# Graph attention: the target term of the scores is written by TensorE, and no longer added to the mask by VectorE

## What is computed

```python
def _L2_gnn_ref(node_features, edge_index, W, a):
    src, tgt = (edge_index[0], edge_index[1])
    h = node_features @ W
    s_src = h @ a[:d_out]
    s_tgt = h @ a[d_out:]
    e = jax.nn.leaky_relu(s_src[src] + s_tgt[tgt], negative_slope=0.2)
    m = jax.ops.segment_max(e, tgt, num_segments=N)
    e_exp = jnp.exp(e - m[tgt])
    denom = jax.ops.segment_sum(e_exp, tgt, num_segments=N)
    attention = e_exp / denom[tgt]
    h_prime = jax.ops.segment_sum(h[src] * attention[:, None], tgt, num_segments=N)
    return jax.nn.elu(h_prime)
...
x = _layernorm(x + _L2_gnn_ref(x, edge_index, L2_gnn_W, L2_gnn_a), axis=-1)
```

## Time and profile before

| | us |
|---|---|
| median of 3 runs (lowest, highest) | 15079.31 (15066.46, 15080.45) |
| the profiled execution, whole | 14940.95 |
| its span in the trace | 14939.1 |
| granted TensorE clock, mean of the span | 0.644 |

### The profile page before, as it was taken

The page is one execution under the profiler, slowest core; times in us unless marked ns, Lnnn a source line. Parts: engine busy times, 40 slices in busy tenths (PEclk is TensorE's granted clock), DMA queues, the critical chain, the costliest instruction groups (busy, mean ns, idle before and its releaser), DMA issues.

```text
span 14939.1 us, 182194 instructions
## 1 busy us (share of the span) xinstructions
PE 8307.1 (56%) x46670; PEld 7582.8 (51%) x46671; DVE 6695.0 (45%) x13205; ACT 2723.1 (18%) x6542; POOL 8996.6 (60%) x8046
## 2 busy tenths in 40 slices
PE   5777787765555555578845555563333334333334
PEld 5777777754445444477745554463333333333333
DVE  6444444434444444489945565564222223222223
ACT  0111111101111111266623333340000000000000
POOL 3888888873556655500037777754666664666664
PEclk7666666666666667799967677775555555555555
DMA  4333333332333333332212222221111111111111
GB/s 91 18 18 18 18 18 18 18 51 68 97 96 98 98 99 96 99 100 98 94 47 66 66 68 67 67 65 27 23 23 23 23 23 26 23 23 23 23 23 23
DMA packets 851085, 769.36 MB, mean 51 GB/s; under 512 B 652784, under 2 KB 660804, under 8 KB 848965
## 3 DMA queue, kind: packets, MB, share of 16 engines
q0 software_dynamic: 446272, 333.87, 16.1%
q1 hardware_dynamic: 249485, 294.83, 5.9%
q10 hardware_dynamic: 155282, 140.11, 3.1%
HBM read 569.49 MB, written 197.82 MB: 51 GB/s over the span
## 4 chain that ended last, share of the span: by engine, by line
issue 23%; another core or an unknown queue 19%; PE 18%; POOL 15%; DVE 10%; DMA 8%; DVEq 5%; ACT 1%; ACTq 0%; POOLq 0%; SPq 0%
POOL lane_tab L679 9%; DMA lane_tab<-rows,idx 7%; POOL tab L703 6%; PE ps L1127 3%; PE ps L1153 3%; PE ps L1128 3%; DVEq L469 2%; DVE acc_w L1797 2%; DVEq L458 1%; DVE buf_d L469 1%; PE ps L1192 1%; PE ps L1178 1%; PE ps L1168 1%; PE ps L1113 1%
## 5 line engine op out<-in xcount | busy, mean ns | idle before, releaser
L703 POOL DMA_INDIRECT tab<-gcn_tab,idx x3136 | 2983.1, 951 | 1807.3 <-issue 1232.9
L679 POOL DMA_INDIRECT lane_tab<-rows,idx x1664 | 2598.3, 1561 | 616.8 <-issue 616.8
L703 POOL DMA_INDIRECT tab<-att_tab,idx x1568 | 1739.2, 1109 | 1923.1 <-DVEq L1684 1311.1
L1168 PE MATMUL ps<-tab,buf_d 128*128 x3328 | 795.2, 387 | 2162.6 <-issue 2121.8
L1168 PEld LDWEIGHTS ps<-tab,buf_d 128*128 128x128 f32 x3328 | 781.0, 320 | 2249.3 <-issue 2249.3
L1797 DVE TENSOR_TENSOR acc_w<-acc_w,ps 128x512 f32 x416 | 286.1, 688 | 3395.9 <-remote 3108.7
L693 POOL DMA_INDIRECT buf_b<-src_tab,idx x832 | 825.6, 992 | 749.4 <-ACT idx L813 296.4
L693 POOL DMA_INDIRECT acc_w<-src_tab,idx x832 | 838.0, 1007 | 598.0 <-ACT idx L813 335.1
L1065 PE MATMUL ps<-ident,srcg 128*128 128x128 f32 x3328 | 721.9, 405 | 659.6 <-DVE srcg L1430 655.1
L1168 PE MATMUL ps<-tab,buf_a 128*128 x3328 | 762.8, 424 | 531.7 <-issue 403.3
L1168 PEld LDWEIGHTS ps<-tab,buf_a 128*128 128x128 f32 x3328 | 725.9, 330 | 650.5 <-issue 650.1
(11 more groups left out here) (283 smaller groups left out, 16942.2 us busy)
## 6 DMA issues: line engine op xcount, KB each, us to landing
y_stash<-buf_c SPq DMA_DIRECT2D x208, 512.0 KB
tab<-y_stash SPq DMA_DIRECT2D x208, 512.0 KB, 3.3
aux<-dst_rows ACTq DMA_DIRECT2D x104, 512.0 KB
buf_b<-dst_rows ACTq DMA_DIRECT2D x104, 512.0 KB
tab<-gcn_tab,idx POOLq DMA_INDIRECT x3136
aux<-in_edge_attr_dram ACTq DMA_DIRECT2D x848, 32.0 KB
aux<-in_edge_attr_dram SPq DMA_DIRECT2D x848, 32.0 KB
lane_tab<-rows,idx POOLq DMA_INDIRECT x1664
```

The lines of the kernel that those rows point to most:

```text
L679: pool.indirect_dma_start(lane_tab[k][:, :], bass.IndirectOffsetOnAxis(ap=idx[:, b, u:u + 1], axis=0), rows[:, b, u, 0:D1], None, compute_ ...
L703: pool.indirect_dma_start(to[k][:, u, :], None, table[:, :], bass.IndirectOffsetOnAxis(ap=idx[:, k % RING, u:u + 1], axis=0)).then_inc(row ...
L1168: last = pe.matmul(ps_flat[:, bass.ds(rel[u] + q * 512, D)], g_hot[q][:, u, :], g_ring[:, bass.ds(at[u], D)], start=False, stop=True, skip ...
```

## The change

VectorE's second pass over the mask (L1696) goes. In its place TensorE writes `t_step` into the two score banks before the scores: two products per group of the identity with the group's `t_step` columns, each column repeated 128 times, 512 columns per product and bank. The 8 products of s_src then add to what is there (`start=False`) in place of overwriting it. The wait for the banks (`l2_masked`) stands ahead of the new products, and the wait for the s_src columns (`l2_columns`) behind them. The mask counts one semaphore step per group where it counted two.

```diff
@@ -1231,10 +1231,15 @@
             last.then_inc(s.l2_targets, 1)
 
             def l2_scores(g, q):
+                pe.wait_ge(s.l2_masked, g + 1)
+                pe.sem_inc(s.passed, 1)
+                for c in range(2):
+                    pe.matmul(ps[:, c, :].rearrange("p (k f) -> p k f", f=P), ident[:, :],
+                              bc(t_step[:, bass.ds(g * G + c * (G // 2), G // 2)].unsqueeze(2), [P, G // 2, P]),
+                              start=True, stop=False, skip_group_check=True)
                 pe.wait_ge(s.l2_columns, g + 1)
-                pe.wait_ge(s.l2_masked, g + 1)
                 for u in range(G):
-                    last = pe.matmul(region(u, P), bc(s_cols[:, q % 2, u:u + 1], [P, P]), ident[:, :], start=True, stop=True)
+                    last = pe.matmul(region(u, P), bc(s_cols[:, q % 2, u:u + 1], [P, P]), ident[:, :], start=False, stop=True, skip_group_check=True)
                 last.then_inc(s.l2_scored, 1)
 
             def l2_turns(g, q):
@@ -1692,8 +1697,6 @@
                 mask = l2_dst[q]
                 dve.wait_ge(dst_in[q], turn * 16 + 16)
                 dve.tensor_scalar(mask, mask, ids[:, 0:1], -MASK, ALU.not_equal, ALU.mult).then_inc(s.l2_edges_masked, 1)
-                dve.wait_ge(s.l2_edges_masked, g * 2 + 1)
-                dve.tensor_tensor(mask, mask, bc(step_slice(t_step, g).unsqueeze(2), [P, G, P]), ALU.add).then_inc(s.l2_edges_masked, 1)
 
             def l2_maxima(i, q):
                 g = i * RING + q
@@ -1707,7 +1710,7 @@
                     ins.then_inc(s.l2_chain, 1)
                     dve.wait_ge(s.l2_chain, i * (RING * KL2) + (q * KL2 + k))
 
-                dve.wait_ge(s.l2_edges_masked, g * 2 + 2)
+                dve.wait_ge(s.l2_edges_masked, g + 1)
                 dve.wait_ge(s.l2_scored, g + 3)
                 dve.wait_ge(s.l2_exps, g + 1)
                 dve.tensor_tensor(score, l2_dst[q], regions(0, P), ALU.add).then_inc(s.l2_masked, 1)
```

## The result

| | before, us | changed, us | changed / before [95% interval] |
|---|---|---|---|
| median (lowest, highest) | 15078.41 (15066.46, 15083.62) | 15120.12 (15112.0, 15167.44) | 1.0055 [1.0037, 1.0074] |
| the profiled execution | 14940.95 | 15120.06 | |
| granted TensorE clock, mean of the span | 0.644 | 0.659 | |

The change made the kernel 0.55% slower, where the prediction had 0.9% faster as the likeliest. 15120 lies inside the range given (14800 to 15230), but on the other side of the time before.

What follows compares the result with a forecast made beforehand. The prediction took attention to be bound by GpSimd's gather time plus a tail of compute. 14940.95 - 142 + 13 = 14812 us, scaled by 1.00926 to 14950 us (forecast 14880 to 15040); the range given was 14800 to 15230.

Steps and rivals of the forecast that it cites:

- The held gathers (-142 us): Attention loop: gathers starting during L1696 take 1.76 us instead of 0.95; removing it takes 142 us off GpSimd's time.
- Compute hides behind GpSimd: Attention's smooth stretches: gathers allow a step-group every 10.2 us, TensorE needs 8.6, so its extra work shows only in the tail.
- The first rival: Attention: without L1696's holds compute starves and GpSimd waits for its ring; +187 us, 15270 us scaled; chance 0.27.
- TensorE's group (8.6 us, bounds 7.5 and 9.2): Attention step-group on TensorE with the wide products: 8.6 us, midway between fully hidden and fully added; 0.9 above 7.74.
- the sequencer goes on while the long products run: TensorE's group: reading the places overlaps the wide products, which fill 2.57 us of idle time and cost nothing; 7.5 us.
- The tail (+13 us): Fifteen step-groups after the attention's last gather, each 0.9 us longer on TensorE: 13 us more.
- VectorE (7.74 to 6.5 us if TensorE could follow): Attention step-group: VectorE saves 1.23 us, 255 us in all, taking the smooth pace to 6.5 us if TensorE followed.
- The moved wait and the register instructions: Attention loop: `l2_masked` releases as before; semaphore increments and two register instructions cost below 0.2 us per group, inside 8.6.
- That more than the sum comes back (14833): Attention: compute seldom catches up, so GpSimd's ring waits shrink 60 us and the tail 55; 14833 us scaled; chance 0.14.
- That waits eat what the holds free, at no change (15093): Attention: GpSimd's freed time goes into waits, or L1696 caused no holds; only the tail's 13 us remain; chance 0.12.
- TensorE at the low clock throughout: Attention: TensorE's groups take 13.4 us at the low clock, +346 us, 15430 us scaled; chance 0.05.
- Scaling by the median: Whole kernel: the profiled-execution forecast of 14812 us times 1.00926, median over profiled time, gives 14950 us.

Runs made afterwards that it cites:

- the addition of zeros: The changed kernel with an addition of zeros to the mask, two SBUF operands, where L1696 stood: 15114.54 us, 1.0053 of the kernel before.
- narrow products: The kernel before, VectorE's addition kept, with the two new TensorE products added at 8 columns each and overwritten by the scores: 13346.27 us, ratio 1.001.

## Why the prediction was wrong

**The held gathers (-142 us): right in mechanism and size, wrong in what it was worth.** In the first profile of before I sorted all 1568 gathers by the VectorE instruction that ran when they started. The 186 that started in L1696 took 1734 ns in the mean, the 185 in L1715 1491 ns, the others 953 ns; in L1713, which reads one operand from PSUM, they took 946. So L1696 held up the gathers by 186 x 0.79 = 147 us. In the changed kernel none is left of the first kind. The busy time fell by 189 us, more than 142, since the gathers that start in L1715 (now L1718) also took less, 1242 ns in the mean; on the chip without starvation the gathers take 139 us less from first to last. So the inference of the Trainium skill ("SBUF — State Buffer", section "Who interferes with whom"), that such a pass doesn't hold up the making of descriptors, does not hold here: 1734 against 946 ns.

**"Compute hides behind GpSimd": the step that failed.** The prediction counted some 830 us of starved or waited time and let it follow the gathers: shorter gathers, shorter starvation. Its ground was that "most are ended only by a full ring, which says that their length follows GpSimd and not the other way". The same fact says the opposite. Compute doesn't come back before GpSimd stands still, so making GpSimd quicker only brings the full ring earlier, and the time that compute needs without disturbance has to be found in GpSimd's waits: 128 to 142 us were enough in the two profiles of the kernel before because the holds gave it the rest; without them 371 to 463 us were needed. The first rival said just this, with a threshold (279 us of starved time, where 830 stood in the trace), a sign to watch (waits over 260 us; they were 431) and a chance of 0.27. Its other sign did not come: TensorE's idle time "until issue" between the first and the last gather fell from 874 to 579 us (on the chips of one kind, 796 to 580), and it was VectorE's that rose, from 145 to 233 us. Nor did its time: it had +187 us, and +42 and +138 were measured. By its own numbers it was past its threshold threefold, and the argument that set this aside was the one above. It should have had the greater chance.

**TensorE's group (8.6 us, bounds 7.5 and 9.2): mis-sized, 9.92 us in the tail.** Timeline of TensorE in the changed kernel behind the last gather, three groups in a row:

```profile
10170.11 0.39 PE L1256 MATMUL ps<-ident_b,zero_b 128*128 128x260 bf16 x2
10172.99 3.24 PE L1261 MATMUL ps<-tab,buf_d 128*128 x16 [2.49 <-issue]
10176.03 1.91 PE L1249 MATMUL ps<-ident,buf_a 128*128 128x128 f32 x8
10177.74 3.17 PE L1237 MATMUL ps<-valid_s,ident 128*128 x4
10180.74 1.95 PE L1242 MATMUL ps<-ident,tmp_c 128*128 128x128 f32 x16
10182.52 0.39 PE L1256 MATMUL ps<-ident_b,zero_b 128*128 128x260 bf16 x2
10182.75 1.97 PE L1261 MATMUL ps<-tab,buf_d 128*128 x16
10184.56 1.05 PE L1249 MATMUL ps<-ident,buf_a 128*128 128x128 f32 x8
10185.44 1.89 PE L1237 MATMUL ps<-valid_s,ident 128*128 x4
10187.17 1.95 PE L1242 MATMUL ps<-ident,tmp_c 128*128 128x128 f32 x16
10188.95 0.39 PE L1256 MATMUL ps<-ident_b,zero_b 128*128 128x260 bf16 x2
...
10199.72 0.39 PE L1256 MATMUL ps<-ident_b,zero_b 128*128 128x260 bf16 x2
```

From clearing to clearing (L1256, two products) it is 12.41, 6.43 and 10.77 us. The middle one has no idle time before the sums, and it is one in four: the next such sums start at 10221.44 and 10261.64 us, and the loop is unrolled by four. In the kernel before it was one in four too (9017.33, 9048.10 and 9079.06 us, 31 us apart, four groups). So the piece that I read as "the sequencer goes on while the long products run" had nothing to do with their length: at 10177.74 the wide products take 3.17 us and no idle time follows, at 10195.06 they take 3.04 and 2.48 us follow. And the wide products themselves cost 1.89 us at the high level, 1.73 from start to start, as worked out (1.7), but the group with them also holds pieces at the low level behind its idle time:

```profile
10162.00:10164.00 2.00, 1.75 (x13) 1.75 (x13) 1.68 (x4) 0.00 (x0) 0.00 (x0) 0.81 0.00 0
10164.80:10166.60 1.80, 1.80 (x11) 1.80 (x11) 1.39 (x3) 0.00 (x0) 0.00 (x0) 0.50 0.00 0
...
10168.40:10170.20 1.80, 1.80 (x18) 1.79 (x17) 0.00 (x0) 1.80 (x7) 0.00 (x0) 1.00 0.80 257
```

(busy table of short stretches, changed kernel, columns as in rows 1.) The engine idles 2.48 us, then starts the sums, is granted 0.81 over them and 0.50 over the transposes, and is back at 1.00 for the scores. A group with idle time and all its work at the high level is 9.2 us by the prediction's upper bound (7.47 and 1.7), and one in the kernel with the addition of zeros took 9.10 (10139.68 to 10148.78 us); with such a piece it takes 10.6 to 12.4, without idle time 6.43. The prediction gave at the high level to every group and so had no bound above 9.2, although the same rows show the other level.

**The tail (+13 us): 31 to 34 measured**, fifteen times 2.2 us; with 0.9 for each group it was 13. Sixteen step-groups stood behind the last gather before the change too, not fifteen: the earlier trace rows end at 10110 us, the sixteenth stands at 10115.5. On the chip without starvation there is no tail of this kind, three step-groups behind the last gather.

**VectorE (7.74 to 6.5 us if TensorE could follow): right in that it couldn't.** Without the wide products and without the addition the period is 7.6 us, by 0.15 us shorter than before, so TensorE's 7.5 was the next bound directly below VectorE's 7.7.

**The moved wait and the register instructions: no cost seen.** TensorE's idle time for the columns (L887) before L1242 is 9.7 us in the whole stage; it was 24.0. The kernel with narrow products has both, and its ratio is 1.001 [0.9991, 1.0029] on its chip.

**The other rivals.** That more than the sum comes back (14833) did not happen on chips with starvation, where waits and tail grew. That waits eat what the holds free, at no change (15093), was near in time and right as far as it went. TensorE at the low clock throughout didn't come: its granted clock over the span rose from 0.644 to 0.659.

**Scaling by the median.** Attention took 131 us more in the profile, the median of that chip rose by 42 us, on another chip by 138. The factor 1.00926 was no property of the kernel: as the convolutions' time says, the profile and the median of the kernel before came from executions that are not alike.

**Left open.** What starves the engines while gathers go out undisturbed, and why on some chips only, no run here shows; nor what makes the counts of `l2_sums` late. Why the addition of zeros brings nothing is argued only. And on a chip without starvation the whole change was run, but neither of its parts alone.

**Which kernel to take.** On chips with starvation the kernel before; on those without the changed one, by 1.2%. None of the kernels tried beats both everywhere.

## What to carry to other kernels

Before an edit frees an engine that issues gathers, look whether the others do their work while it issues or while it stands; where they work only in its pauses and stalls, those are supply, and freeing it moves its time into waits. If stretches end only with a full ring, ask whether the producer is the bound at all, however busy it is. Price an engine's group over as many groups as the loop is unrolled, at both clock levels that its rows show, and compare a small gain on more than one chip. Before two profiles are compared, compare a stage in them that the change leaves alone.

## What the runs showed of the hardware

- **The kernel before took from 13304 to 15078 us on different chips**, with the same program. What differs is idle time in which the profile shows nothing to wait for: in TensorE's L1168 37.6 us or over 2100. The gathers of the two convolutions take 3963 to 3965 us on the quick chips, 4576 to 4578 and 4601 to 4602 on the others, whichever kernel runs.
- **TensorE's last product of a group counts its semaphore up late where there is starvation**: over 1 us after its end in 123 of 203 events (the longest 11.7 us), in none of 204 without starvation, and in 14 of 171 where GpSimd pauses.
- **A VectorE pass with two SBUF operands holds up a gather that starts in it**, by 0.79 us in the mean (two different operands, 186 gathers) or 0.55 us (the same one twice, 185 gathers; 0.30 in the changed kernel), and one with an SBUF and a PSUM operand, or a reduction with a single operand, does not (946 ns). The pass itself is not slowed measurably (1.22 to 1.23 us in all of these).
- **Such a hold can be worth more than it costs** (the kernel without it was 0.41 to 0.8% slower on chips with starvation). A pause that GpSimd makes by itself, by waiting for a short instruction of its own, took 1.1 to 1.3 us beyond the usual distance of two gathers, where a hold takes 0.6 to 0.8; with a clearing of 66 columns in place of 528 it is 0.7 to 0.9.
- **A float32 product of 512 columns** takes two passes of 0.43 us at the high level of the clock and 0.85 at the low one. The reading of 17 registers ahead of the sums leaves TensorE idle in three groups of four: 1.2 to 2.6 us in a smooth stretch of the kernel before, 2.4 to 2.5 in the tail of the changed one, and 2.9 to 3.2 ahead of the wide products when it is put there. Behind one such gap the granted clock was 0.81 over the sums, 0.50 over the transposes and 1.00 again over the scores.
